# A loop for masked attention's sequences, and another order for TensorE and ScalarE in the middle pass

## The reference, cut to what matters

```
x = x + attention(norm(x))                      # 16 heads of 64
x = x + softmax(q k^T / 16) v, from the context # one head of 256, weights rounded
x = x + W2[g] (W1[g] xn + b1[g]) + b2[g]        # g = the sequence: 8 pairs of products, no activation between
x = x + experts(...)                            # gate, top 2 of 8, gather, two products, scatter
x = x + masked attention to the context         # 16 heads of 16, 64 keys, a mask on the keys
x = x + quantised pair(norm(x))
```

## Time and profile before

| | us |
|---|---|
| median of 3 runs | 2373.59 |
| lowest, highest | 2372.21, 2380.17 |
| the profiled execution | 2368.86 |
| its span, first to last instruction | 2367.1 |
| middle pass, in the trace | about 1110 to 1370 |
| masked attention, in the trace | about 1823 to 2197 |

### The profile page before, as it was taken

One profiled execution on the slowest core, in us unless ns is written; L12 is line 12 of the kernel. 1 busy time (PEld: TensorE's weight loads), 2 busy tenths in 40 slices (PEclk: granted clock), 3 DMA queues, 4 the chain that ended last, 5 costly groups with the idle time before them and its releaser, 6 DMA issues. The chain is left out here.

```text
span 2367.1 us, 42843 instructions
## 1 busy us (share of the span) xinstructions
PE 1715.8 (72%) x13321; PEld 1084.2 (46%) x13338; DVE 1550.3 (65%) x3111; ACT 1394.6 (59%) x2215; POOL 788.3 (33%) x749
## 2 busy tenths in 40 slices
PE   3789998989999898985888802122443788888577
PEld 1455555555555555553666601121222355555323
DVE  6877777777777777775233386744774675755775
ACT  3889888898979898991444412443553332323745
POOL 0534545454545455450000050470001444443000
PEclk9999999999999999996789955555766787878699
DMA  5222222222222222222122111332102201111001
GB/s 180 61 53 62 59 55 64 61 53 62 62 50 64 59 64 53 64 46 97 36 72 72 36 76 53 122 109 89 54 27 70 81 25 30 23 32 18 1 10 63
DMA packets 173822, 140.04 MB, mean 59 GB/s; under 512 B 83794, under 2 KB 155399, under 8 KB 173366
## 3 DMA queue, kind: packets, MB, share of 16 engines
q1 hardware_dynamic: 166710, 122.78, 19.4%
q0 software_dynamic: 6912, 14.71, 2.7%
HBM read 61.92 MB, written 20.97 MB: 35 GB/s over the span
## 5 line engine op out<-in xcount | busy, mean ns | idle before, releaser
L577 ACT ACTIVATE a_p_hi<-ps,a_probs_up,a_s_scale 128x512 f16<-128x512 f32 x512 | 397.7, 777 | 54.9 <-ACTq L575 54.1
L689 DVE TENSOR_REDUCE a_top<-ps 128x2 f32<-128x1024 f32 x256 | 313.1, 1223 | 132.6 <-DVEq L688 132.6
L578 ACT ACTIVATE a_probs<-ps,a_probs_up,a_s_scale 128x512 f32<-128x512 f32 x512 | 398.5, 778 | 0.0
L917 POOL TENSOR_TENSOR a_p_lo<-a_probs,a_p_hi 128x1024 f16<-128x1024 f32 x128 | 277.8, 2170 | 210.4 <-POOLq L916 169.1
L905 POOL TENSOR_TENSOR a_ops<-a_ident_down,a_top 64x256 f16<-64x256 f32 x256 | 158.9, 621 | 340.8 <-POOLq L900 332.3
L698 DVE TENSOR_TENSOR a_p_lo<-a_probs,a_p_hi 128x1024 f16<-128x1024 f32 x128 | 182.7, 1427 | 41.2 <-DVEq L697 41.2
L441 PE MATMUL ps<-a_ops 128*128 128x512 f16 x512 | 195.8, 382 | 17.7 <-PEq L439 17.6
L460 PE MATMUL ps<-a_v_hi,a_p_hi 128*128 128x65 f16 x2048 | 205.6, 197 | 2.1 <-PEq L455 2.0
L463 PE MATMUL ps<-a_v_lo,a_p_hi 128*128 128x64 f16 x2048 | 205.6, 195 | 0.0
L464 PE MATMUL ps<-a_v_hi,a_p_lo 128*128 128x65 f16 x2048 | 205.5, 196 | 0.0
L460 PEld LDWEIGHTS ps<-a_v_hi,a_p_hi 128*128 128x128 f16 x2048 | 191.2, 99 | 23.0 <-issue 11.1
(11 more groups left out here) (487 smaller groups left out, 3767.3 us busy)
## 6 DMA issues: line engine op xcount, KB each, us to landing
a_ops<-a_qk SPq DMA_DIRECT2D x384, 128.0 KB, 2.3
f_w<-in_L_ffn_W_dram SPq DMA_DIRECT2D x16, 1024.0 KB, 7.6
a_qd<-a_qk SPq DMA_DIRECT2D x128, 64.0 KB, 2.2
g_a<-in_L_attn_gp_w_dram SPq DMA_DIRECT2D x8, 1024.0 KB
X<-in_x_dram SPq DMA_DIRECT2D x8, 512.0 KB, 9.9
expert_in<-g_w SPq DMA_DIRECT2D x8, 512.0 KB
g_a<-in_L_attn_dp_w_dram SPq DMA_DIRECT2D x8, 512.0 KB
e_x_in<-expert_in SPq DMA_DIRECT2D x8, 512.0 KB, 4.3
```

What stands on the lines that cost most here:

```text
L577: nc.scalar.activation(p_hi[:, h % 2, k, :], scores, ACT.Exp, bias=probs_up[:], scale=s_scale[:])
L578: nc.scalar.activation(probs[:, h % 2, k, :], scores, ACT.Exp, bias=probs_up[:], scale=s_scale[:]).then_inc(st_taken, 1)
L689: nc.vector.tensor_reduce(top[:, c % 2, 2 * pair:2 * pair + 2], ps[:, ROW:ROW + 2, :], AX.X, ALU.max).then_inc(row_taken, 1)
L917: nc.gpsimd.tensor_tensor(p_lo[:, h % 2, 2:KT, :], probs[:, h % 2, 2:KT, :], p_hi[:, h % 2, 2:KT, :], ALU.subtract).then_inc(p_made_pool, 1)
```

## The change

There are two parts, with nothing in common but the kernel. In the middle pass `f_rows(b - 1)` moves in front of `scores(b + 1)` and of the second half of W2, in the bank list and on PE; on ACT `f_rows_out(b - 1)` moves in front of the last two copies of W2. In masked attention the seven equal sequences become the body of a `Fori` on each of POOL, PE, ACT and DVE; `b` is then a register, in addresses, slices and the counts that are waited for.

```diff
         for b in range(B + 1):
             if b < B:
                 in_order += [("pT", b), ("w2T", b, 0), ("w2T", b, 1)]
+            if b:
+                in_order += [("f_rows", b - 1, 0), ("f_rows", b - 1, 1)]
             if b + 1 < B:
                 in_order += [("scores", b + 1)]
             if b < B:
-                in_order += [("w2T", b, 2), ("w2T", b, 3)]
-            if b:
-                in_order += [("f_rows", b - 1, 0), ("f_rows", b - 1, 1)]
-            if b < B:
-                in_order += [("av", b, 0), ("av", b, 1)]
+                in_order += [("w2T", b, 2), ("w2T", b, 3), ("av", b, 0), ("av", b, 1)]
...
                         turn_w2(b, 0)
                         turn_w2(b, 1)
+                    if b:
+                        for c in range(DC):
+                            f_rows(b - 1, c)
                     if b + 1 < B:
                         scores(b + 1, bank_of["scores", b + 1])
                     if b < B:
                         turn_w2(b, 2)
                         turn_w2(b, 3)
-                    if b:
-                        for c in range(DC):
-                            f_rows(b - 1, c)
-                    if b < B:
                         values(b, 0)
                         values(b, 1)
...
                         w2_out(b, 0)
                         w2_out(b, 1)
+                    if b:
+                        for c in range(DC):
+                            f_rows_out(b - 1, c)
                     if b < B:
                         w2_out(b, 2)
                         w2_out(b, 3)
-                    if b:
-                        for c in range(DC):
-                            f_rows_out(b - 1, c)
...
-                for b in range(B - 1):
+                with pool.Fori(0, B - 1) as b:
...
-                for b in range(B - 1):
+                with pe.Fori(0, B - 1) as b:
                     sequence(b, more=True)
...
-                for b in range(B - 1):
+                with act.Fori(0, B - 1) as b:
                     sequence(more=True)
...
-                for b in range(B - 1):
+                with dve.Fori(0, B - 1) as b:
                     sequence(b, more=True)
                     dve.drain()
```

## The result

The changed kernel takes 2348.68 us (median of four runs, 2344.94 to 2350.14) against 2372.9 for the kernel before: 0.990 of its time, 95% interval 0.9859 to 0.9941. The prediction had 2369.1 and a range from 2350. The profiled execution took 2350.14 us, with a span of 2348.4 against 2367.1. DVE, ACT and POOL are as busy as before, within 2 us; PE does the same 13321 products in 1697.3 us instead of 1715.8. What changed is how long TensorE runs at 2.4 GHz.

What follows compares the result with a forecast made beforehand. No engine was taken to bound the whole; PE's waits and clock mattered in the middle pass, mostly PE's chain in masked attention. 2368.86 - 9.5 + 5 = 2364.4 us profiled, 2369.1 as median; range 2350 to 2390.

Steps and rivals of the forecast that it cites:

- Middle pass, the waits: Middle pass, PE: a new wait of 2.2 us ahead of f_rows, and none left ahead of outputs.
- The gain apart from the clock: Middle pass: outputs starts at 1238.1 instead of 1239.4, 1.3 us gained a turn.
- Clock up, -3.3 a turn: Middle pass, clock staying up: 1.3 us from the earlier outputs plus 2.0 from outputs at 2.4 GHz.
- Clock down, +3.5, in two turns of six: Middle pass: clock falls around the new wait, turn 3.5 us worse than now; expected in two of six turns.
- Sum of the middle pass, -9.5: Middle pass: two turns at +3.5, four at -3.3 and the seventh at -3.3 us; ends -23 and +17.7.
- Masked attention, the loop's own price, 1.3 us a sequence: Masked attention: PE's branch 0.4, DVE's registers 0.4 and 0.4, PE's registers 0.1 us; 9 us for seven sequences.
- Code that needn't be loaded, at 0: Masked attention: removing six of seven code copies gains 0, at most 1.5 us, as nothing visibly waited for loading.
- Some comes back ... I take half: Masked attention: later work meets the higher clock earlier, so half the 9 us returns; +5 us, ends -1.5 and +20.
- Rival 1: Middle pass: the clock never falls; -23 + 5 = -18 us, 2355.6 us in all; chance 0.22.
- Rival 2: Middle pass: the clock falls in four turns or more; +9 to +23 us, 2382 to 2396; chance 0.15.
- Rival 3: Masked attention: the loop costs more, by exposed DVE register waits (2380) or PE's body reloaded each turn (+18, 2387); chance 0.20.

Runs made afterwards that it cites:

- e13: Changed kernel with products whose result is overwritten in TensorE's waits in masked attention (also the 0.87 us one) and in the middle pass; 2318.78 us (0.9767).
- e15: As e13, but the middle pass in its order before the change, with its products in the wait ahead of outputs; 2329.35 us (0.9818).
- e1: Kernel before the change with the new order of the middle pass alone; 2365.48 us (0.9973).
- e7: Changed kernel with three products whose result is overwritten in TensorE's longest wait in masked attention; 2344.13 us (0.9899).
- e10: As e7, with one more overwritten product ahead of each of three short waits: last outputs' transposes, last projection, last addition to x; 2335.93 us (0.9849).
- e14: As e13, but with masked attention's sequences written out on all engines instead of loops; 2316.32 us (0.9753).
- e3: Kernel before the change with only TensorE's (PE's) sequences of masked attention as a loop; 2372.25 us (0.9989).
- e2: Kernel before the change with the four loops of masked attention alone; 2353.96 us (0.9926).
- e9: Kernel before the change, written out, with two operations on an unawaited semaphore ahead of each addition of the mask on DVE; 2353.69 us (0.9926).
- e6: Kernel before the change with only ACT's and POOL's sequences of masked attention as loops; 2367.34 us (0.9977).
- e11: Changed kernel with two overwritten products ahead of f_rows in the middle pass (not in turn 8) and two ahead of outputs in the last turn; 2333.95 us (0.9832).
- e5: Kernel before the change with only DVE's sequences of masked attention as a loop; 2353.81 us (0.9935).

## Why the prediction was wrong

- *Middle pass, the waits.* Right. 2.2 us forecast ahead of `f_rows`, 2.06 to 2.24 measured; none ahead of `outputs`. The gain apart from the clock, forecast at 1.3 us a turn, is 1.1 to 1.3 (e13 against e15).
- *Clock up, -3.3 a turn.* Right: -3.46, -2.64, -3.34, -3.54, and -3.29 in turn 8.
- *Clock down, +3.5, in two turns of six.* Right in kind and, by luck, in number: two fell, at +3.68 and +5.60; the range's two ends had none and six. The second costs more because the old order had only 1.41 us of wait in that turn. That the number isn't the code's property is shown by the traces with the same code: one such turn in e1, two in e7 and e10.
- *Sum of the middle pass, -9.5.* Too large by a third or less: -2.8 in the one pair of traces, but -6.4 by e1's runs and -7.1 by the means of twelve traces. What the pair lacks beside the turns, +2.82 in the last and +1.35 ahead of the second, is the old order's too in most of its traces. The prediction's fault here is to take the clock of the one trace it had, in which the last turn stays up, for the kernel's.
- *Masked attention, the loop's own price, 1.3 us a sequence.* Right: 1.0 (e13 against e14). Code that needn't be loaded, at 0: no gain from it shows, in e3 or in e14.
- *"Some comes back ... I take half".* This is the step that failed. The clock was held to be a discount on the time added, so that it could at most return what the loop cost; the range of the term ended at -1.5. In fact the clock's second fall in every sequence, 10.2 us at half speed, hung on a few tenths of a us of DVE's chain. Forecast +5, measured -16.5 in the trace and -17.6 by e2's runs. The clock row, 0.79, had been read as a constant of the stage; its falls inside a sequence were never laid out, though PE's own rows showed two of them: 3.62 us for the scores, and 1.94 for eight transposes at the next sequence's start, which take 1.06 at 2.4 GHz.
- *Rivals.* None was it. Rival 1's total, 2355.6, was the nearest, for another reason: the clock did fall in the middle pass. Rival 2 wanted four turns or more with a fall and the traces have one or two. Rival 3's reloading doesn't occur. The Trainium skill, "Runtime: NRT & Kernel Launch", "Instruction fetch mechanics", has a taken branch stall when its target has left the loaded pages; with PE's loop the idle time at the sequence's end grew by 0.55 us in all, and q8 loaded no block over six sequences (e3), where it had loaded eight, so PE's body isn't loaded anew in each turn and no such stall is seen here.

How the delay works can be followed so far. PE waits for DVE's divisions 3.65 us in the kernel before, 3.78 after, 4.01 in e9. The clock falls within this wait in all three. Behind it the scores begin 2.3 us after the fall before the change (1988.10 to 1990.35), 3.0 after (2020.10 to 2023.08) and 2.7 in e9 (1988.00 to 1990.72). The clock rises 6.8 us after its fall in each. So from the rise to the start of the values the old kernel has 0.3 us of its projection left, e9 0.5 and the changed one 0.7, and then each has one set of values and four transposes before PE waits. In the old kernel the clock fell again at 1998.37; in the other two it didn't.

The traces of all ten kernels without added products in masked attention (before, after, e1 to e6, e9, e11) bear this out. In 62 of their sequences the long wait holds a fall of 6.8 us. In the 26 in which the scores begin 1.55 to 2.35 us after that fall, a second one of 10.2 us follows 10.2 us after the first; in the 36 in which they begin 2.41 to 3.67 us after it, none follows there. e3 stands at the border: 2.33 to 2.35 us in its second to fifth sequences, with a second fall behind each, and 2.51 in the sixth, with none. This is why PE's loop alone, whose delay lies elsewhere, loses just one of the falls, the one between its last two sequences. That the lateness decides is shown by e9 and e5; that it decides by way of how much work is left behind the rise is my reading, not tested by itself.

The Trainium skill, "TensorE: Matmul & The Clock Gate", "HAM oscillation — how this bites in real kernels", describes a kernel in which a wait in each step brings the clock down, so that each step begins cold, and mends it by a loop order that does more products ahead of each wait. Here the same is seen at 40.9 us a sequence with two falls; that it can also be mended by products put into the waits is what e10 to e13 show: against the changed kernel e13's middle pass is 17.4 us shorter (238.53 against 255.96) and its six sequences 10.3.

## What to carry to other kernels

Lay out the granted clock inside one period of each repeated stage before pricing a change there: where it falls, which wait it falls in, and what runs at half speed behind it. If it falls in every period, a term of both signs as large as those slow stretches belongs in the range of any edit that moves work by tenths of a us, and a measured gain may say nothing about the edit. Take more than one trace before calling a turn's clock the kernel's: the same middle pass took 249.2 and 256.0 us here. Then fill TensorE's waits with products that nobody reads, and only with the clock held judge the edit by itself.

## What the runs showed of the hardware

- Two semaphore operations on DVE (they start 0.09 us apart, and the idle time ahead of the mask's addition grows from 0.19 to 0.37 us), three times on a chain of 41 us, made a sequence 3.4 us shorter on average (e9).
- In this stage, scores that began 2.35 us or less after the fall of the clock in TensorE's long wait were followed by a second fall in 26 sequences of 26, and by none where they began 2.41 us or more after it, in 36 of 36.
- Products of 512 columns in the waits (three of them, six records, take 2.74 us) held the clock at 1.00 through 159 us of the middle pass (e11) and through sequences of 36.1 us (e13; in one of its six it still fell, for 3.4 us); a fall of 3.4 us that began right behind a wait of 0.87 us cost a sequence 1.4 to 1.8 us (e10).
- The loops' price on the chip: TensorE's COMPARE_BRANCH 76 to 225 ns, in the rows below, and 0.55 us of idle time in all at the sequence's end; DVE's counter instructions 0.1 us where it waits for them. With PE's loop q8 loaded no instructions over six sequences (e3), in place of eight blocks.

```profile
L2651 PEldq COMPARE_BRANCH  x7: 76/208/225, 1919.3 to 2147.3; - x7
```
